# Six layers of local attention: the query copy split by PSUM banks, and the output product added to the tokens ahead of the norm floor

## The reference

```python
for i in range(6):
    x = attn_layer(shift_tokens(x), Wqkv[i], q_scale[i], k_scale[i], Wo[i]) + x
    x = ffn_layer(shift_tokens(x), ...) + x
def attn_layer(x, Wqkv, qs, ksc, Wo):
    q, k, v = split(x @ Wqkv)               # 16 heads of 64
    q, k = l2norm(q) * qs, l2norm(k) * ksc  # t / max(|t|, 1e-12)
    q, k = rotary(q), rotary(k)
    out = local_attention(q, k, v)          # windows of 32, keys of this and the last window
    return out @ Wo
```

## Time and profile before

| | |
|---|---|
| median of 3 runs | 4221.26 us (4219.84 to 4221.34) |
| the profiled execution, its own time | 4222.04 us |
| its span, first to last instruction | 4220.2 us |
| granted TensorE clock, mean | 0.99 |
| TensorE matmul busy | 3945.5 us, 93% |
| TensorE weight load busy | 2740.2 us, 65% |
| VectorE busy | 3868.1 us, 92% |
| ScalarE busy | 2606.7 us, 62% |
| GpSimd busy | 2696.9 us, 64% |

### The profile page before, as it was taken

How to read it: one execution, slowest core, us unless ns; L and a number is a source line. 1 busy time by engine, 2 the same in 40 slices (tenths; PEclk the granted TensorE clock), 3 DMA queues, 4 the chain that set the end, 5 groups by cost and what they waited for, 6 DMA issues and landing times. The chain is left out here.

```text
span 4220.2 us, 124486 instructions
## 1 busy us (share of the span) xinstructions
PE 3945.5 (93%) x48616; PEld 2740.2 (65%) x48616; DVE 3868.1 (92%) x4452; ACT 2606.7 (62%) x3780; POOL 2696.9 (64%) x4716
## 2 busy tenths in 40 slices
PE   7999999997999999999999999999999999999996
PEld 5666666665666666666666666666666666666664
DVE  5888888887999999999999999999999999999994
ACT  4666666653566666666666665666666666666663
POOL 5565556645667676676667666666676666766663
PEclk9999999999999999999999999999999999999998
DMA  5454554540000011000110001100011000010000
GB/s 136 93 100 95 98 98 92 103 99 20 24 17 15 20 29 29 17 15 17 32 29 16 16 16 31 28 18 15 16 30 30 18 15 16 20 39 18 15 16 14
DMA packets 342439, 165.07 MB, mean 39 GB/s; under 512 B 114240, under 2 KB 337472, under 8 KB 341184
## 3 DMA queue, kind: packets, MB, share of 16 engines
q1 hardware_dynamic: 342208, 161.99, 17.2%
HBM read 115.67 MB, written 33.69 MB: 35 GB/s over the span
## 5 line engine op out<-in xcount | busy, mean ns | idle before, releaser
L630 POOL TENSOR_TENSOR pn<-es,rden 128x1024 f32<-128x1024 f32 x192 | 366.6, 1909 | 695.7 <-DVE rden L958 695.7
L726 ACT ACTIVATE y<-ps 128x1024 f32<-128x1024 f32 x384 | 372.3, 1021 | 503.8 <-PE ps L1204 503.8
L634 POOL TENSOR_TENSOR t<-t 128x1024 f32<-128x1024 f32 x192 | 454.7, 2368 | 69.0 <-DVE t L911 69.0
L678 ACT ACTIVATE t<-ps,amx 128x512 f32<-128x512 f32 x512 | 347.9, 689 | 224.5 <-DVE amx L815 224.5
L909 DVE TENSOR_TENSOR t<-ps,tabl 128x1024 f32<-128x1024 f32 x384 | 467.1, 1216 | 7.8 <-ACT sq L749 4.6
L911 DVE TENSOR_TENSOR t<-ps,tabl 128x1024 f32<-128x1024 f32 x384 | 466.4, 1215 | 0.0
L636 POOL TENSOR_TENSOR t<-t 128x1024 f32<-128x1024 f32 x192 | 453.3, 2361 | 4.7 <-DVE t L911 4.7
L1012 DVE TENSOR_TENSOR qn<-t,rn 128x2048 f32<-128x2048 f32 x192 | 438.1, 2282 | 5.0 <-POOL rn L399 5.0
L968 DVE TENSOR_REDUCE ss<-sq 128x32 f32<-128x2048 f32 x192 | 437.0, 2276 | 0.0
L1053 PEld LDWEIGHTS ps<-cst,qn 128*128 128x128 f32 x3072 | 350.2, 141 | 116.5 <-issue 64.2
L815 DVE TENSOR_REDUCE amx<-ps 128x2 f32<-128x1024 f32 x256 | 311.0, 1215 | 111.3 <-PE ps L1075 111.0
(11 more groups left out here) (134 smaller groups left out, 8245.4 us busy)
## 6 DMA issues: line engine op xcount, KB each, us to landing
wm<-values_dram SPq DMA_DIRECT2D x128, 256.0 KB, 5.0
y<-values_dram SPq DMA_DIRECT2D x128, 256.0 KB, 4.7
values_dram<-qT SPq DMA_DIRECT2D x64, 256.0 KB, 2.3
tokens_dram<-x SPq DMA_DIRECT2D x96, 128.0 KB
xs<-tokens_dram SPq DMA_DIRECT2D x192, 64.0 KB, 1.8
xw<-tokens_dram SPq DMA_DIRECT2D x192, 64.0 KB, 1.9
xsh<-x SPq DMA_DIRECT2D x48, 128.0 KB
xsh<-x SPq DMA_DIRECT2D x48, 127.0 KB
```

Of the source, the lines that this page charges most:

```text
L630: nc.gpsimd.tensor_tensor(heads(pn[:], H), heads(es[:], H), rden[:].unsqueeze(2).to_broadcast([P, H, KEYS]), ALU.mult).then_inc(l_p, 1)
L634: nc.gpsimd.tensor_tensor(t1[:, 0:INNER], t1[:, 0:INNER], t2[:, 0:INNER], ALU.add).then_inc(l_rotq, 1)
L726: return act.activation(y[:].rearrange("p h (w q) -> p w h q", w=NW)[:, 2 * half:2 * half + 2], src.rearrange("p (w h q) -> p w h q", w=2, ...
```

## The change

ScalarE copies `qT` in two instructions of 128x512, one for each bank of pool0, and waits before each for its own four transposes; TensorE's q transposes signal after four and after eight. `l_tq` and `l_qT` then grow by two a turn. The output product, which writes bank 0, waits for the first half only (count 2t+5); what writes bank 1 or reads all of `qT` waits for both (2t+6). On VectorE the add of the output product moves from behind the guess (and, in c=0, behind the statistics) to right behind the sums of squares, ahead of the floor.

```diff
--- before.py
+++ after.py
@@ -741,9 +741,11 @@
                     past(act, l_ss, t + 3)
                     act.activation(sq[:, 0:INNER], pool3, ACT.Square).then_inc(l_sqq, 1)
                 if s.has(2):
-                    act.wait_ge(l_tq, t + 3)
                     past(act, l_s, t + 2)
-                    act.activation(qT[:].rearrange("p h c -> p (h c)"), pool0, ACT.Copy).then_inc(l_qT, 1)
+                    for half in range(2):
+                        act.wait_ge(l_tq, 2 * t + 5 + half)
+                        act.activation(qT[:, 4 * half:4 * half + 4].rearrange("p h c -> p (h c)"), bank(half),
+                                       ACT.Copy).then_inc(l_qT, 1)
                 if s.has(3):
                     act.wait_ge(l_pk, t + 4)
                     act.activation(sq[:, INNER:2 * INNER], pool1, ACT.Square).then_inc(l_sqk, 1)
@@ -966,6 +968,11 @@
                     dve.wait_ge(l_sqk, t + 4)
                     rotate(1, u, pool1, l_rk)
                     nc.vector.tensor_reduce(ss[:], heads(sq[:], 2 * H), X, ALU.add).then_inc(l_ss, 1)
+                if s.has(0):
+                    dve.wait_ge(l_o, t + 1)
+                    xb = x[:, bass.ds((s.b * NU + c) * DIM, DIM)]
+                    nc.vector.tensor_tensor(xb, xb, ps_o, ALU.add).then_inc(l_x, 1)
+                if s.has(3):
                     dve.wait_ge(l_ss, t + 4)
                     nc.vector.tensor_tensor(ss[:], ss[:], floor_const[:], ALU.max).then_inc(l_fl, 1)
                     dve.wait_ge(l_fl, t + 4)
@@ -973,10 +980,6 @@
                                             ALU.mult, ALU.add).then_inc(l_gs, 1)
                 if c == 0 and s.ffn(1):
                     statistics(s.f1)
-                if s.has(0):
-                    dve.wait_ge(l_o, t + 1)
-                    xb = x[:, bass.ds((s.b * NU + c) * DIM, DIM)]
-                    nc.vector.tensor_tensor(xb, xb, ps_o, ALU.add).then_inc(l_x, 1)
                 if s.has(1):
                     dve.wait_ge(l_p, t + 2)
                     past(dve, l_y, t + 1)
@@ -1048,8 +1051,8 @@
                                          wqkL[v][:, i * INNER + s * 512:i * INNER + (s + 1) * 512], start=True, stop=True)
                 return m
 
-            def transposes(i, pool, src):
-                for a in range(PAIRS):
+            def transposes(i, pool, src, half=None):
+                for a in range(PAIRS) if half is None else range(half * 4, half * 4 + 4):
                     t = nc.tensor.transpose(pool[:, a * P:(a + 1) * P], src[:, i * INNER + a * P:i * INNER + (a + 1) * P], ident)
                 return t
 
@@ -1250,14 +1253,15 @@
                     past(pe, l_y1sb, t + 1)
                     if s.has(3):
                         past(pe, l_xT, t + 4)
-                    transposes(0, pool0, qn[:]).then_inc(l_tq, 1)
+                    for half in range(2):
+                        transposes(0, pool0, qn[:], half).then_inc(l_tq, 1)
                     past(pe, l_y0sb, t + 1)
                     transposes(1, pool2, qn[:]).then_inc(l_tk, 1)
                 if s.has(0):
                     pe.wait_ge(l_y0sb, t + 1)
                     pe.wait_ge(l_y1sb, t + 1)
                     if s.has(2):
-                        pe.wait_ge(l_qT, t + 3)
+                        pe.wait_ge(l_qT, 2 * t + 5)
                     if s.turn_of(0, 0):
                         pe.wait_ge(s_msb, (s.l + 1) * NU)
                     for odd in range(2):
@@ -1267,11 +1271,11 @@
                 if part is not None:
                     n, v, q = part
                     if s.has(2):
-                        pe.wait_ge(l_qT, t + 3)
+                        pe.wait_ge(l_qT, 2 * t + 6)
                     past(pe, l_xT, t + 4)
                     fold(n, q)
                 if s.turn_of(1, 1):
-                    pe.wait_ge(l_qT, t + 3)
+                    pe.wait_ge(l_qT, 2 * t + 6)
                     ffn_bias(s.l)
                 if s.has(3):
                     pe.wait_ge(l_rq, t + 4)
```

## The result

The changed kernel takes **4199.46 us** as the median of 5 runs (4192.4 to 4201.41), against 4221.26 (4219.84 to 4224.25) for the kernel before on the same chip: ratio 0.9945, 95% interval 0.993 to 0.9959. So it is 22 us faster, where 59 were forecast and the range ended at 4198. The profiled execution took 4192.4.

A forecast was written before the change was run, and what follows sets the result against it. TensorE and VectorE were nearly full, three loops closing at nearly one length. Gains of 0.20 + 0.50 + 0.27 + 0.27 = 1.24 us a batch, x 48 = 59.5, gave 4162 us; range 4148 to 4198.

The forecast's parts named there:

- Edit 1, the query copy: TensorE before the output product: the wait for ACT's `qT` copy vanishes, product starts 0.50 us earlier; ACT pays 0.17 more.
- the objection of the Trainium skill to small tiles: ACT's query copy: the fixed PSUM cost is paid twice, halves cost 0.14 us more; decides only if ACT were the bound.
- Edit 2, the add: VectorE: add hidden while GpSimd's addition holds the floor; `pT` 0.13 us earlier in c=2 and c=3, 0.20 in c=0.
- The lag of the windows behind `pT`: TensorE in c=2 and c=3: where windows wait for `pT`, they start 0.13 us after its end.
- c=0: `pT`, windows, `y`, exponential, `den` all move by 0.20: c=0 turns, where statistics make VectorE late: the whole chain behind the add comes 0.20 us earlier.
- the sum: Gain per batch of four turns: 0.20 + 0.50 + 0.27 + 0.27 = 1.24 us.
- 48 equal batches: Layers: 192 turns as 48 batches of four, each gaining 1.24 us, 59.5 us in all.
- 1 (the lag of 0.32 everywhere): Windows on TensorE answer `pT` as late as in c=0: 0.52 a batch, 25 us gain, 4197; chance 0.12.
- 2 (the add not hidden): VectorE: add held by GpSimd's L636, or floor needs its time after it: 28 us gain, 4194; chance 0.10.
- 3 (the stuck root step decides c=1): GpSimd: one more root step stuck behind `qn` holds c=1's floor: 16 us less gain, 4178; chance 0.08.
- 4 (the gap stays): TensorE's gap before the output product stays, only c=0 gives 0.20: 10 us gain, 4212; chance 0.06.
- 5 (register waits): TensorE's changed wait counts no longer share a register: 0.46 us a turn, slower, 4250; chance 0.04.

The follow-up runs named there:

- e1: Changed kernel with the add moved back behind guess and statistics, so only the query copy is split: 4207.01 us, ratio 0.9963 to the kernel before.
- e2: Kernel before with only the add moved ahead of the floor, query copy whole: 4210.78 us, ratio 0.9975.
- e3: Changed kernel plus two unused matmuls in c=0 turns (except each layer's second batch), ahead of the windows' wait for `pT`: 4155.89 us.
- e5: Changed kernel with the FFN's statistics in c=0 moved from ahead of `pT` to right behind it on VectorE: 4161.42 us, ratio 0.9853.

## Why the prediction was wrong, by its steps

**Edit 1, the query copy: right, and a little more.** 0.50 less was forecast from transposes to product; 2.25 became 1.74. ACT's two halves cost it 0.06 of span (1.09 against 1.03, as they overlap) and nobody waits for them, so the objection of the Trainium skill to small tiles (VectorE: DVE Perf Modes, The TRN2 errata), by which the halves cost 0.14 more, stayed without weight, as said. Not foreseen: the 32 products now last 3.74 instead of 3.81 with no wait in front. 0.50 + 0.07 is the 0.57 that c=1 gave.

**Edit 2, the add: right in kind, undersized.** It is hidden under the held floor, which still ends 0.05 behind L636. `pT` then starts 0.09 to 0.10 after the guess in c=2, where I took 0.21 out of 0.13 to 0.21: the 0.21 between add and `pT` belonged to the add and went with it. So `pT` is 0.24 earlier in the turn and not 0.13, and c=2 and c=3 give 0.38 and 0.39, not 0.27. In c=0 the same: `pT` now follows the last statistic at 0.11 (2404.75 to 2404.86), where in e1 statistic, add and `pT` stand 0.21 and 0.21 apart; 0.31 went in place of 0.20.

**The lag of the windows behind `pT`: right.** 0.13 in c=2 and c=3, 0.32 in c=0.

**The step that failed: "c=0: `pT`, windows, `y`, exponential, `den` all move by 0.20", and with it the sum, which took every duration of TensorE from rows at full clock.** The sum made TensorE 0.50 earlier in front of the hole and `pT`, which ends it, 0.20: by its own terms the hole of 1.62 had to grow to 1.92. (The runs show 0.65 more by the split, e1, and 0.32 less by the add, e2, and 1.97 with both.) I had the row and read it as slack. It is a risk: behind the longer hole the clock falls, and `y` comes 3.71 after the windows' start in place of 2.14. No term of the sum, no bound and none of the five rivals had the clock in it.

The balance, from the second `den` to that of the last batch (187 turns): before 3098.5, e3 3035.0, 63.5 less. The 30 regular batches give 46.3 of it. 25 give about 1.67 each where 1.24 was forecast. The five of the last layer give only 0.95: there VectorE has one more add in c=1 (L998, 0.69 long, the sum with the other branch), and c=1 takes 17.01 in e3 in place of 16.24:

```profile
3836.11 0.65 DVE L994 TENSOR_TENSOR x<-x,ps 128x512 f32 x1
3836.88 0.69 DVE L998 TENSOR_TENSOR x<-x,wm  x1
3837.49 1.22 DVE L1005 TENSOR_REDUCE mx<-ps 128x16 f32<-128x1024 f32 x1
```

The prediction took 48 equal batches and has no term for that. The other 67 turns (with folding, loads of weights and the ends of layers) give 17.2, 1.03 for four of them. So the forecast of 59.5 was near what the two edits are worth, by errors of opposite sign, which is luck.

The changed kernel takes 3069.7 in the same stretch: 28.8 less than before, 34.7 more than e3. 28.8 of the 34.7 lie in the 20 regular batches with a fall, at about 1.65 each (0.87 in the last layer, where VectorE ends c=1 anyway), 5.9 in the other turns: there are falls in c=0 there too, and in three of the turns with the wait for `b1s` the clock stays low for 6.8 in place of 3.4 (the turn takes 23.1 against 21.6 to 21.95 in e3). So the clock took more than half of what the edits are worth.

**The rivals.** 1 (the lag of 0.32 everywhere): no, 0.13 in c=2. 2 (the add not hidden): no. 3 (the stuck root step decides c=1): not in the changed kernel, where the floor of c=1, in turns without a fall, went from 1.21 to 1.40 without lengthening the turn; in e5, with GpSimd pushed back further, it did, by 0.25. 4 (the gap stays): no. 5 (register waits): no. That 4199 lies near the times of rivals 1 and 2 is chance.

**What stays open.** Why the clock falls in 20 of 30 batches at a hole of 1.97, in 11 of 30 at 2.28 and in none at 1.62 (before) and 1.30 (e2). The falls come in a row: in four layers the fourth to sixth batch, in the first the fifth to seventh, in the last all five. Either something that doesn't run with the turns decides it, or what TensorE does around the hole; no run here separates the two. The clock records lean to the first: within such a row of falls the starts lie 64.85 apart (1751.34, 1816.19 and 1881.05 in the second layer), while the holes lie 65.08 apart, so each fall starts sooner behind its hole (0.70, 0.49, 0.25), and then the row ends. What can be said of the length: in regular batches no hole up to 1.62 had a fall behind it, and three of the five falls of the kernel before follow holes of 1.97 to 2.06 in other turns. The Trainium skill (TensorE: Matmul & The Clock Gate, What's actually happening) calls the low level the default and says that activity releases the throttle. The rows agree in direction, as more work gave more clock; here the engine was 94% busy over the span, so the share on the page is no protection.

## What to carry to other kernels

When an edit makes TensorE earlier and what it waits for not as much, the sum needs a line for the clock: take each hole of TensorE in the trace, add what the edit makes of it, and price one fall (here 1.65 us a batch) in any turn where the hole grows beyond those after which the granted clock is seen to stay (here it stayed at 1.62 and didn't at 1.97). And look for kinds of turns in which another engine has more work, as in the last layer here, before multiplying one gain by all turns. After the change the clock of the runs is the first thing to compare; if it dropped, fill or close the hole before judging the edit. A small instruction held by another engine is a free slot: five instructions were put ahead of such a floor without moving its end.

## What was not expected of the hardware

- One or two more matmuls in every fourth turn, whose result nobody uses, made the kernel 44 to 46 us faster (4155.89 and 4152.96 against 4199.46), and nothing faster where the clock had held (4222.06 against 4221.23).
- The clock fell when TensorE was already at work again: in the turn shown, between 2406 and 2407, after a hole that ended at 2406.42. So with 22 of the 23 falls in c=0 of the changed kernel, 0.21 to 1.44 behind the hole; but one began inside a hole of 2.76, and in e1 5 of 17 did, at most 0.33 before its end.
- A longer hole had fewer falls (2.28: 11 of 30; 1.97: 20 of 30), and the kernel with more idle time in all, in shorter holes, had none in its regular batches (3.03 a batch before, 2.15 after).
- The floor as an operation with one tensor and an immediate is held by GpSimd's addition for as long as the form with two tensors (1.35, to 0.03 behind it).
